# A mixture-of-experts step whose up product is turned over: stationary weights, moving rows, h born transposed

## The chip, the cores and the metric

The kernel runs on one core of a Trainium2 chip. The metric is the device time of one execution in microseconds. The times shown are the median of three runs; one more execution was profiled.

## What is computed

A decoder layer on x of shape (8, 256, 256) in three parts, each behind a layer norm and each added to x: a gated projection, a cross attention with a decay mask (retention), and a mixture of experts. The change touches the last part alone:

```python
xn = rms_norm(layernorm(x), norm_scale)              # 2048 tokens of 256
scores = xn @ w_router.T                             # 8 experts
ids = top_k(scores, 2); c = softmax(scores)[ids]
h = xn @ w_up[e].T                                   # 256 -> 1408, value and gate of 704
h = h_value * silu(h_gate)
y = h @ w_down[e].T                                  # 704 -> 256
out = x + sum over the 2 experts of y * c
```

## The kernel before

The stages run one after the other: stage A (projection), stage B (attention, norms, router scores, and beside them the scaling and splitting of the expert weights), the routing, and stage E, the experts. Stage E gathers the (token, expert) pairs, sorted by expert, into NSLOT = 39 tiles of 128 rows. All rows of a tile have one expert, whose number stands in `tile_e` and is only known on the chip.

Numbers are kept as a high and a low fp16 part. A product of two such numbers is made of three products (high by high, high by low, low by high); the list `products` holds them for the two halves c of the 256 inputs, so there are six matmuls for one output.

Stage E is a software pipeline, written out by hand for each engine in a function `step_e(it, k, r)`. `steps` unrolls steps 0 to 5 and 38 to 41, and puts steps 6 to 37 into a hardware loop whose body holds two steps (`E_STEPS`). In step r the up product is that of tile r-1, the down product that of tile r-2, and the y copy that of tile r-3. For one tile:

- GpSimd gathers the rows with an indirect DMA (L716), SyncE's queue transposes them with a DMA into `xsT`, which has two slots (L423).
- TensorE, up product (`up`, L1221): the transposed rows `xsT` are the stationary operand, the expert's weights `up_w` the moving one. Three groups fill bank 0 (gate, 512 columns), bank 1 (value, 512) and bank 2 (the last 192 gate and the last 192 value columns, 384). Each group is six matmuls. The rows of h come out on the partitions.
- ScalarE takes the silu of the gate (L608, L624), VectorE multiplies with the value (L1035), ScalarE makes the high fp16 part (L620, L626), VectorE the low one (L1041, L1043, L1044).
- TensorE transposes h in 11 pieces of 128x128 (L1251) into banks 4 and 5. VectorE copies eight of them (L1021) and ScalarE three (L614) to `hT`.
- TensorE, down product (L1276 to L1280): pieces of `hT` are stationary, the down weights `dn_w` moving, 256 columns, 17 matmuls in bank 7. Piece c has three products; the low part of the last 64 rows shares its piece with the high part.
- ScalarE scales y with the pair's weight (L602), and GpSimd adds it to the output with an indirect DMA (L726).

On TensorE the order within step r is: up group 0 of tile r-1, the transposes of tile r-2, up groups 1 and 2 of tile r-1, the down product of tile r-2.

Of the kernel before, what the change touches and what calls it, by code (L numbers as in the profile page):

```python
# [13 lines left out]
P = 128  # L14
NBATCH = 8
SEQ = 256
D = 256
# [40 lines left out]
def build(nc, x, ctxT, wproj, wproj2, w1, w2, gbias, wq, wk, wv, nscale, wr, wup, wdn, consts, consts_b, consts2, xrow_hbm, out):  # L58
# [5 lines left out]
    with ctx:  # L64
# [119 lines left out]
        def rt(n):  # L184
# [28 lines left out]
        sg = view(arena, 1728, H)  # L213
        hh = view(arena, 2432, H)
        hT = view(arena, 3136, H).bitcast(fp16).rearrange("p (c n) -> p c n", c=NHS)
        yt = view(arena, 3904, 2, D)
        hs = view(arena, 4416, H).bitcast(fp16)
        hs_high, hs_low_tail, hs_low4, hs_low = hs[:, 0:H], hs[:, H:H + HLAST], hs[:, H + HLAST:H + HLAST + P], hs[:, 2 * H - HA:2 * H]
        pair_scale = view(arena, 5120, NSLOT)
# [57 lines left out]
        s_trh, s_hTa, s_hTb = sem("h_transposed"), sem("hT_first_bank_ready"), sem("hT_second_bank_ready")  # L277
# [4 lines left out]

        hT_bank = [bank[4][:, :].bitcast(fp16).rearrange("p (c n) -> p c n", n=P),
                   bank[5][:, 0:3 * P // 2].bitcast(fp16).rearrange("p (c n) -> p c n", n=P)]
# [141 lines left out]
        def _(act):  # L426
# [165 lines left out]
            def step_e(it, k, r):  # L592
# [3 lines left out]
                if live(r, 3, NSLOT):  # L596
                    i, _, slot = at(it, k, 3)
                    act.wait_ge(s_y, i + 1)
                    act.wait_ge(s_ps, i + 1)
                    if r >= 5:  # L600
                        act.wait_ge(s_add, 16 * i - 16)
                    nc.scalar.activation(yt[:, slot], bank[7][:, 0:D], ACT.Copy, scale=pair_scale[:, ds(i, 1)]).then_inc(s_yt, 1)  # L602
                if live(r, 1, NSLOT):
# [4 lines left out]
                    nc.scalar.activation(sg[:, 0:HA], bank[0][:, 0:HA], ACT.Silu, scale=descale[:, ds(e, 1)]).then_inc(s_sg, 1)  # L608
                if live(r, 2, NSLOT):
                    i, _, _ = at(it, k, 2)  # L610
                    act.wait_ge(s_trh, i + 1)
                    if r >= 3:
                        act.wait_ge(s_y, i)
                    nc.scalar.activation(hT[:, 8:NHS], hT_bank[1], ACT.Copy).then_inc(s_hTb, 1)  # L614
                if live(r, 1, NSLOT):
                    i, _, slot = at(it, k, 1)
                    act.wait_ge(s_h, 2 * i + 1)
                    if r >= 2:
                        act.wait_ge(s_trh, i)
                    nc.scalar.activation(hs_high[:, 0:HA], hh[:, 0:HA], ACT.Copy).then_inc(s_hhi, 1)  # L620
# [3 lines left out]
                    nc.scalar.activation(sg[:, HA:H], bank[2][:, 0:HB], ACT.Silu, scale=descale2[:, ds(e, 1)]).then_inc(s_sg, 1)  # L624
                    act.wait_ge(s_h, 2 * i + 2)
                    nc.scalar.activation(hs_high[:, HA:H], hh[:, HA:H], ACT.Copy).then_inc(s_hhi, 1)  # L626
# [107 lines left out]
        def _(dve):  # L734
# [270 lines left out]
            V.tensor_copy(descale2, descale).then_inc(s_ysc, 1)  # L1005
            down_low(DN_TABLE, DN_GATHER)
            dve.wait_ge(s_ysc, 4)

            def step_e(it, k, r):
# [6 lines left out]
                if live(r, 2, NSLOT):  # L1016
                    i, _, _ = at(it, k, 2)
                    dve.wait_ge(s_trh, i + 1)
                    if r >= 3:
                        dve.wait_ge(s_y, i)  # L1020
                    V.tensor_copy(hT[:, 0:8], hT_bank[0]).then_inc(s_hTa, 1)  # L1021
# [5 lines left out]
                if live(r, 1, NSLOT):  # L1027

                    i, _, _ = at(it, k, 1)
                    for q, (src, cols) in enumerate(((bank[1][:, 0:HA], slice(0, HA)), (bank[2][:, HB:2 * HB], slice(HA, H)))):  # L1030
                        dve.wait_ge(s_sg, 2 * i + q + 1)
                        dve.wait_ge(s_up, 3 * i + q + 2)
                        if r >= 2:
                            dve.wait_ge(s_hlo, 2 * i + q - 1)
                        V.scalar_tensor_tensor(out=hh[:, cols], in0=src, scalar=h_scale[:, ds(e_h, 1)], in1=sg[:, cols],  # L1035
                                               op0=ALU.mult, op1=ALU.mult).then_inc(s_h, 1)
                        dve.wait_ge(s_hhi, 2 * i + q + 1)
                        if r >= 2 and q == 0:
                            dve.wait_ge(s_trh, i)
                        if q == 0:  # L1040
                            V.tensor_tensor(hs_low, hh[:, cols], hs_high[:, cols], ALU.subtract).then_inc(s_hlo, 1)  # L1041
                        else:
                            V.tensor_tensor(hs_low4, hh[:, HA:HA + P], hs_high[:, HA:HA + P], ALU.subtract)  # L1043
                            V.tensor_tensor(hs_low_tail, hh[:, HA + P:H], hs_high[:, HA + P:H], ALU.subtract).then_inc(s_hlo, 1)  # L1044
                    if r == 1:
                        down_low(DN_GATHER, 2 * NE)
# [4 lines left out]
        def _(pe):  # L1051
# [322 lines left out]
```

## Time and profile before

| | us |
|---|---|
| median of 3 runs | 443.6 (439.12 to 444.65) |
| the profiled execution, device time | 439.83 |
| its span, first to last instruction | 438.0 |
| first up matmul of stage E, from the span's start | 184.0 |
| TensorE busy | 365.9 (84% of the span) |
| VectorE busy | 269.9 (62%) |
| ScalarE busy | 236.5 (54%) |
| GpSimd busy | 191.2 (44%) |

The profile is that of one execution. Its span leaves out 1.8 us of the device time, which lie before the first and behind the last instruction. [...] Weight loads (PEld) run beside the matmuls. [...]

### The profile page before, as it was taken

What the parts mean: (1) busy time and instruction counts of PE and PEld (TensorE: products, weight loads), DVE (VectorE), ACT (ScalarE), POOL (GpSimd) and SP (SyncE); (2) the same over time, 40 slices, a digit from 0 to 9 for tenths busy, and PEclk for the clock granted to TensorE, in tenths of its full rate; (3) what the DMA queues carried; (4) which work ended last, traced back from release to release, by engine and by line L of the source; (5) the groups of instructions that cost most, each with busy time, mean ns of one, the idle gap of its engine ahead of it and who ended that gap; (6) DMA issues with size and microseconds to landing.
All of it is one profiled execution on the core that took longest, in us unless ns stands there. A gap on an engine that the chain in (4) does not pass through costs nothing.

```text
span 438.0 us, 9733 instructions
## 1 busy us (share of the span) xinstructions
PE 365.9 (84%) x2444; PEld 263.8 (60%) x2445; DVE 269.9 (62%) x688; ACT 236.5 (54%) x434; POOL 191.2 (44%) x186
## 2 busy tenths in 40 slices
PE   0899999788996411289999999999999999999980
PEld 0678888677885311056666666666666666666650
DVE  3698879978788899854445544455444554445530
ACT  3699877876765660534453444444445344444430
POOL 2544445866667413214333443334433444433321
PEclk9999999999998555599999999999999999999996
DMA  8999943352213170224343433434334343343420
GB/s 237 399 426 403 347 134 97 96 193 73 72 49 96 49 198 0 49 49 53 61 75 61 73 60 61 73 61 73 58 63 73 61 73 60 61 72 61 62 24 12
DMA packets 45859, 47.02 MB, mean 107 GB/s; under 512 B 26256, under 2 KB 41616, under 8 KB 44816
## 3 DMA queue, kind: packets, MB, share of 16 engines
q1 hardware_dynamic: 38304, 36.28, 26.5%
q0 software_dynamic: 7536, 10.52, 15.0%
q8 instruction: 8, 0.13, 0.1%
q14 instruction: 11, 0.09, 0.1%
HBM read 32.17 MB, written 9.50 MB: 95 GB/s over the span
## 4 chain that ended last, share of the span: by engine, by line
PE 70%; DVE 12%; issue 4%; ACT 4%; DMA 4%; SPq 1%; POOL 1%; DVEq 0%; ACTq 0%; POOLq 0%
PE bank L1225 32%; PE bank L1251 5%; PE bank L1276 5%; PE bank L1277 5%; PE bank L1278 5%; PE bank L1105 3%; PE bank L1153 3%; PE bank L1162 2%; DMA expert_w<-in_wup 2%; PE bank L1117 2%; ACT arena L438 2%; DVE expert_w L827 2%; DVE expert_w L836 1%; DVE arena L982 1%; PE bank L1058 1%
## 5 line engine op out<-in xcount | busy, mean ns | idle before, releaser
L1225 PE MATMUL bank<-expert_w,arena 128*128 x702 | 153.5, 364 | 8.8 <-DMA arena<-arena 8.6
L726 POOL DMA_INDIRECT out<-arena,add_idx x39 | 61.7, 1583 | 132.4 <-ACT arena L602 132.4
L1225 PEld LDWEIGHTS bank<-expert_w,arena 128*128 128x128 f16 x702 | 67.5, 98 | 68.0 <-issue 12.6
L1021 DVE COPY arena<-bank 128x1024 f16<-128x1024 f16 x39 | 27.0, 692 | 55.4 <-PE bank L1251 55.3
L620 ACT ACTIVATE arena<-arena 128x512 f16<-128x512 f32 x39 | 24.6, 630 | 64.8 <-DVE arena L1035 64.8
L1035 DVE SCALAR_TENSOR_TENSOR arena<-bank,dn_small,arena 128x512 f32<-128x512 f32 x78 | 45.4, 582 | 21.2 <-PE bank L1225 17.3
L1276 PE MATMUL bank<-expert_w,arena 128*128 x195 | 53.2, 273 | 1.3 <-DVE arena L1021 0.9
L1277 PE MATMUL bank<-expert_w,arena 128*128 x195 | 53.2, 273 | 0.0
L1278 PE MATMUL bank<-expert_w,arena 128*128 x195 | 53.2, 273 | 0.0
L716 POOL DMA_INDIRECT arena<-xrow_hbm,take_idx x39 | 38.9, 998 | 24.5 <-issue 11.5
L1041 DVE TENSOR_TENSOR arena<-arena 128x512 f16<-128x512 f32 x39 | 27.0, 693 | 27.1 <-ACT arena L620 27.1
L681 POOL TENSOR_TENSOR arena<-arena 128x512 f32<-128x512 f32 x16 | 27.0, 1689 | 21.4 <-DVE arena L864 15.5
L1251 PEld LDWEIGHTS bank<-ident,arena 128*128 128x128 f16 x429 | 27.1, 98 | 11.2 <-ACT arena L626 2.5
L602 ACT ACTIVATE arena<-bank,arena 128x256 f32<-128x256 f32 x39 | 18.5, 474 | 25.1 <-issue 20.6
L608 ACT ACTIVATE arena<-bank,small 128x512 f32<-128x512 f32 x39 | 26.8, 688 | 9.7 <-PE bank L1225 9.0
L827 DVE SCALAR_TENSOR_TENSOR expert_w<-expert_w,small 128x1408 f16<-128x1408 f32 (+1 forms) x16 | 30.3, 1893 | 2.6 <-ACT expert_w L483 1.2
L1251 PE MATMUL bank<-ident,arena 128*128 128x128 f16 x429 | 30.3, 219 | 1.8 <-DVE arena L1044 1.0
L626 ACT ACTIVATE arena<-arena 128x192 f16<-128x192 f32 x39 | 14.1, 363 | 30.3 <-DVE arena L1035 30.3
L1058 PE MATMUL bank<-cst,arena 128*128 128x128 f32 x96 | 16.7, 302 | 14.3 <-ACT arena L453 10.3
L507 ACT ACTIVATE expert_w<-expert_w,dn_small 128x768 f16<-128x768 f32 x16 | 14.7, 931 | 18.2 <-DVE expert_w L836 17.8
L438 ACT ACTIVATE arena<-expert_w,front 128x1408 bf16<-128x1408 f32 x16 | 23.7, 1479 | 1.0 <-DMA expert_w<-in_wup 0.8
L1058 PEld LDWEIGHTS bank<-cst,arena 128*128 128x128 f32 x96 | 12.4, 154 | 18.9 <-issue 11.3
(176 smaller groups left out, 673.5 us busy)
## 6 DMA issues: line engine op xcount, KB each, us to landing
expert_w<-in_wup SPq DMA_DIRECT2D x8, 1408.0 KB, 17.1
expert_w<-in_wdn SPq DMA_DIRECT2D x10, 640.0 KB, 5.0
rows<-in_x SPq DMA_DIRECT2D x8, 256.0 KB, 7.0
arena<-in_ctxT SPq DMA_DIRECT2D x8, 256.0 KB, 3.1
xrow_hbm<-front SPq DMA_DIRECT2D x8, 256.0 KB, 2.2
out<-rows SPq DMA_DIRECT2D x8, 256.0 KB, 2.8
expert_w<-in_wdn SPq DMA_DIRECT2D x20, 64.0 KB, 4.9
cst_b<-in_consts_b SPq DMA_DIRECT2D x1, 960.0 KB, 12.4
```

The lines of the kernel that those rows point to most:

```text
L438: nc.scalar.activation(squares, raw_chunk(e * 2 + c), ACT.Square, scale=ns_s[:, c:c + 1], accum_out=sq[:, ds(e * 2 + c, 1)]).then_inc(s_sq, 1)
L681: nc.gpsimd.tensor_tensor(dst[:, slot], dst[:, slot], rot[:, n], ALU.add).then_inc(rotated, 1)
L716: pool.indirect_dma_start(out=xs_row[:, i % 2], out_offset=None, in_=xrow_hbm, in_offset=bass.IndirectOffsetOnAxis(ap=take_idx[:, i:i + 1] ...
L726: pool.indirect_dma_start(out=out, in_=yt[:, i % 2], in_offset=None, out_offset=bass.IndirectOffsetOnAxis(ap=add_idx[:, i:i + 1], axis=0), ...
L827: V.scalar_tensor_tensor(out=part(n, 1), in0=raw_chunk(n), scalar=up_scale[:, ds(n, 1)], in1=part(n, 0), op0=ALU.mult, op1=ALU.subtract).t ...
L1035: V.scalar_tensor_tensor(out=hh[:, cols], in0=src, scalar=h_scale[:, ds(e_h, 1)], in1=sg[:, cols], op0=ALU.mult, op1=ALU.mult).then_inc(s_ ...
L1058: last = T.transpose(dst[:, c * SEQ + j * P:c * SEQ + (j + 1) * P], src(j, c), ident)
L1225: last = T.matmul(bank[q][:, 0:n], xsT[:, slot, 2 * a + c], up_w[:, ds(w0 + c * UPC + w * 2 * H + lo, n)], start=m == 0, stop=m == len(pro ...
L1251: last = T.transpose(hT_bank[c // 8][:, c % 8], hs[:, c * P:(c + 1) * P], ident16[:, :])
L1276: T.matmul(y, hT[:, c], dn_at(w_dn, c, 0), start=c == 0, stop=False)
L1277: T.matmul(y, hT[:, c], dn_at(w_dn, c, 1), start=False, stop=False)
L1278: T.matmul(y, hT[:, NH if c == NH - 2 else NH + 1 + c], dn_at(w_dn, c, 0), start=False, stop=False)
```

## The change

The up product is turned over. A tile of 128 weight columns of `up_w` is now the stationary operand, and the 128 rows of `xsT` move. Each output is 128 columns of h (on the partitions) by 128 rows, so h comes out transposed. There are twelve outputs for one tile: four in the gate bank, four in the value bank, and four in the third bank (128 gate columns, the last 64 gate columns, 128 value columns, the last 64 value columns), each of six matmuls as before. The transposes, banks 4 and 5 as their place, and the two copies out of them go. The high and low parts are written right into `hT`, which now has two slots. The up banks have two slots (0 to 2 and 3 to 5), y has two banks (6 and 7). The silu and the high part of the third bank take 256 columns in place of 192 (their last 64 partitions hold zeros or are not used). VectorE handles the last 128x192 product as one of 128x128 and one of 64x128, and the low part of the last tile is written to partitions 64 to 127. TensorE's order in step r becomes: all up groups of tile r-1, then the down product of tile r-2. The numbers of the computation and the weights' layout in memory are the same.

```diff
-            def up(i, slot, w0, q, lo, n, between=None):
+            def up_tile(q, slot, w0, t, columns):
                 for m, (c, a, w) in enumerate(products):
-                    if m == 3 and between:
-                        between()
-                    last = T.matmul(bank[q][:, 0:n], xsT[:, slot, 2 * a + c],
-                                    up_w[:, ds(w0 + c * UPC + w * 2 * H + lo, n)],
-                                    start=m == 0, stop=m == len(products) - 1)
-                last.then_inc(s_up, 1)
+                    weights = columns(w0 + c * UPC + w * 2 * H)
+                    last = T.matmul(bank[3 * slot + q][0:weights.shape[1], t * P:(t + 1) * P], weights,
+                                    xsT[:, slot, 2 * a + c], start=m == 0, stop=m == len(products) - 1)
+                return last
+
+            def whole(lo):
+                return lambda w0: up_w[:, ds(w0 + lo, P)]
+
+            def tail(lo):
+                return lambda w0: up_w[:, ds(w0 + lo + P, HLAST)]
...
-                    if r >= 2:
-                        pe.wait_ge(s_h, 2 * i - 1)
-                    up(i, slot, w_up, 0, 0, HA)
+                    if r >= 3:
+                        pe.wait_ge(s_h, 2 * i - 2)
+                    for q in range(2):
+                        for t in range(HA // P):
+                            last = up_tile(q, slot, w_up, t, whole(q * HA + t * P))
+                        last.then_inc(s_up, 1)
+                    if live(r, 2, NSLOT):
+                        load_expert("down", at(it, k, 2)[0], 2 * DNC)
+                    for t, columns in enumerate((whole(2 * HA), tail(2 * HA), whole(2 * HA + HB), tail(2 * HA + HB))):
+                        last = up_tile(2, slot, w_up, t, columns)
+                    last.then_inc(s_up, 1)
                 if live(r, 2, NSLOT):
-                    i, _, _ = at(it, k, 2)
-                    pe.wait_ge(s_hhi, 2 * i + 2)
-                    pe.wait_ge(s_hlo, 2 * i + 2)
-                    if r >= 3:
-                        pe.wait_ge(s_hTa, i)
-                        pe.wait_ge(s_hTb, i)
-                    for c in range(NHS):
-                        last = T.transpose(hT_bank[c // 8][:, c % 8], hs[:, c * P:(c + 1) * P], ident16[:, :])
-                    last.then_inc(s_trh, 1)
...
-                    pe.wait_ge(s_hTa, i + 1)
-                    pe.wait_ge(s_hTb, i + 1)
-                    if r >= 3:
-                        pe.wait_ge(s_yt, i)
-                    y = bank[7][:, 0:D]
+                    pe.wait_ge(s_hhi, 2 * i + 2)
+                    pe.wait_ge(s_hlo, 2 * i + 2)
+                    if r >= 4:
+                        pe.wait_ge(s_yt, i - 1)
+                    y = bank[6 + slot][:, 0:D]
```

On ScalarE and VectorE:

```diff
-                    nc.scalar.activation(hT[:, 8:NHS], hT_bank[1], ACT.Copy).then_inc(s_hTb, 1)
...
-                    nc.scalar.activation(hs_high[:, 0:HA], hh[:, 0:HA], ACT.Copy).then_inc(s_hhi, 1)
+                    nc.scalar.activation(hT_high[slot][:, 0:HA], hh[:, 0:HA], ACT.Copy).then_inc(s_hhi, 1)
...
-                    nc.scalar.activation(sg[:, HA:H], bank[2][:, 0:HB], ACT.Silu, scale=descale2[:, ds(e, 1)]).then_inc(s_sg, 1)
+                    nc.scalar.activation(sg[:, HA:NH * P], bank[3 * slot + 2][:, 0:2 * P], ACT.Silu,
+                                         scale=descale2[:, ds(e, 1)]).then_inc(s_sg, 1)
...
-                    V.tensor_copy(hT[:, 0:8], hT_bank[0]).then_inc(s_hTa, 1)
...
+                    V.scalar_tensor_tensor(out=hh[:, whole], in0=bank[3 * slot + 2][:, 2 * P:3 * P], scalar=h_scale[:, ds(e_h, 1)],
+                                           in1=sg[:, whole], op0=ALU.mult, op1=ALU.mult)
+                    V.scalar_tensor_tensor(out=hh[0:HLAST, tail], in0=bank[3 * slot + 2][0:HLAST, 3 * P:4 * P],
+                                           scalar=h_scale[0:HLAST, ds(e_h, 1)], in1=sg[0:HLAST, tail],
+                                           op0=ALU.mult, op1=ALU.mult).then_inc(s_h, 1)
...
+                    V.tensor_tensor(hT_low[slot][:, whole], hh[:, whole], hT_high[slot][:, whole], ALU.subtract)
+                    V.tensor_tensor(hT[HLAST:P, slot, NH - 1], hh[0:HLAST, tail], hT[0:HLAST, slot, NH - 1],
+                                    ALU.subtract).then_inc(s_hlo, 1)
```

## Rows read from the trace of the kernel before

**Rows 1.** The page, parts 1 and 2: TensorE's busy time; its clock in 40 slices
```profile
PE 365.9 (84%) x2444; PEld 263.8 (60%) x2445; DVE 269.9 (62%) x688; ACT 236.5 (54%) x434; POOL 191.2 (44%) x186
...
PEclk9999999999998555599999999999999999999996
```

**Rows 2.** Windows: stretch and length, busy us (instructions) by engine, PEclk, DMA, GB/s
```profile
70.00:80.00 10.00, 7.57 (x39) 6.08 (x37) 9.57 (x23) 6.84 (x9) 6.74 (x7) 1.00 0.01 2
...
130.00:140.00 10.00, 7.03 (x41) 6.11 (x41) 9.13 (x20) 5.48 (x8) 7.56 (x8) 0.99 0.33 105
140.00:150.00 10.00, 4.29 (x18) 3.34 (x16) 8.86 (x15) 4.98 (x10) 6.55 (x6) 0.50 0.15 52
...
210.00:400.00 190.00, 189.59 (x1442) 125.33 (x1441) 91.65 (x217) 88.22 (x188) 79.98 (x63) 1.00 0.38 66
```

**Rows 3.** Groups of instructions, 210 to 400 us: count, busy us, mean ns, idle before
```profile
L1225 PE MATMUL bank<-expert_w,arena 128*128 x563 | 122.1, 362 | 0.0
L1225 PEld LDWEIGHTS bank<-expert_w,arena 128*128 128x128 f16 x562 | 53.6, 98 | 45.9 <-issue 1.1
...
L1251 PE MATMUL bank<-ident,arena 128*128 128x128 f16 x352 | 24.9, 219 | 0.0
...
L1021 DVE COPY arena<-bank 128x1024 f16<-128x1024 f16 x31 | 21.4, 692 | 46.6 <-PE bank L1251 46.6
...
L614 ACT ACTIVATE arena<-bank 128x384 f16<-128x384 f16 x31 | 15.0, 483 | 0.0
```

**Rows 4.** Timeline of one step, 300.3 to 306.5 us: start, length, what, how many
```profile
300.46 1.46 PE L1225 MATMUL bank<-expert_w,arena 128*128 x6
...
301.75 0.78 PE L1251 MATMUL bank<-ident,arena 128*128 128x128 f16 x11
...
302.37 2.43 PE L1225 MATMUL bank<-expert_w,arena 128*128 x12
...
304.63 0.27 PE L1276 MATMUL bank<-expert_w,arena 128*128 x1
...
306.38 0.27 PE L1280 MATMUL bank<-expert_w,arena 128*128 x1
...
306.49 1.46 PE L1225 MATMUL bank<-expert_w,arena 128*128 x6
```

**Rows 5.** Line L1225, 183.8 to 185.4 us: count, min/median/max ns, first and last start
```profile
L1225 PEldq FUSED_REGOPS  x12: 46/46/46, 183.9 to 185.3; - x12
...
L1225 PE MATMUL bank<-expert_w,arena x4: 606/634/634, 184.0 to 185.3; 128*128 x4
```

**Rows 6.** Line L1276, 305.1 to 305.8 us, the down product within the step of rows 4
```profile
L1276 PEldq FUSED_REGOPS  x3: 46/46/46, 305.1 to 305.6; - x3
L1276 PEld LDWEIGHTS bank<-expert_w,arena x2: 95/96/98, 305.2 to 305.5; 128*128 128x128 f16 x2
```

**Rows 7.** Lines L1225, L1276, L1279 and L1280, 210 to 400 us
```profile
L1225 PEldq FUSED_REGOPS  x375: 46/46/51, 210.1 to 400.0; - x188
...
L1276 PEldq FUSED_REGOPS  x155: 46/46/60, 212.2 to 395.7; - x155
...
L1279 PEldq FUSED_REGOPS  x31: 46/46/46, 213.5 to 395.9; - x31
...
L1280 PE MATMUL bank<-expert_w,arena x31: 272/273/273, 215.0 to 397.7; 128*128 x31
```

**Rows 8.** L1219, 304.2 to 305.2; then L1219, L1249, L310, 210 to 400 us
```profile
L1219 PEldq FUSED_REGOPS  x2: 46/98/151, 304.3 to 304.8; - x2
...
L1219 PEldq TENSOR_LOAD <-arena x63: 297/303/630, 210.3 to 399.3; - x63
...
L1249 PEldq EVENT_SEMAPHORE  x31: 51/485/507, 215.6 to 398.3; - x31
...
L310 PEldq COMPARE_BRANCH  x15: 207/208/220, 225.8 to 396.3; - x15
```

**Rows 9.** Line L1280 over the whole span: the last matmul of the kernel
```profile
L1280 PE MATMUL bank<-expert_w,arena x39: 272/273/273, 196.9 to 426.4; 128*128 x39
```

More of the change, by code:

```diff
@@ L212, in build @@
         xsT = view(arena, 1120, 2, 2 * P).bitcast(fp16).rearrange("p s (c n) -> p s c n", c=4)
[L213 to L219, printed above, removed]
+        sg = view(arena, 1728, NH * P)
+        hh = view(arena, 1728 + NH * P, NH * P)
+        hT = view(arena, 1728 + 2 * NH * P, 2 * H).bitcast(fp16).rearrange("p (s c n) -> p s c n", s=2, c=NHS)
+        hT_low = [hT[:, s, NH:NHS].rearrange("p c n -> p (c n)") for s in range(2)]
+        hT_high = [hT[:, s, 0:NH].rearrange("p c n -> p (c n)") for s in range(2)]
+        o = 1728 + 2 * NH * P + 2 * H
+        yt = view(arena, o, 2, D)
+        pair_scale = view(arena, o + 2 * D, NSLOT)
+        assert o + 2 * D + NSLOT <= 5840 and (NH - 1) * P + HLAST == H
         bank = [ctx.enter_context(nc.psum_tensor(f"bank{i}", [P, 512], fp32)) for i in range(8)]
@@ L276, in build @@
         s_hhi, s_hlo = sem("h_high_ready"), sem("h_low_ready")
-        s_trh, s_hTa, s_hTb = sem("h_transposed"), sem("hT_first_bank_ready"), sem("hT_second_bank_ready")
         s_y, s_yt = sem("y_ready"), sem("y_copied")
@@ L601, in step_e @@
                         act.wait_ge(s_add, 16 * i - 16)
-                    nc.scalar.activation(yt[:, slot], bank[7][:, 0:D], ACT.Copy, scale=pair_scale[:, ds(i, 1)]).then_inc(s_yt, 1)
+                    nc.scalar.activation(yt[:, slot], bank[6 + slot][:, 0:D], ACT.Copy, scale=pair_scale[:, ds(i, 1)]).then_inc(s_yt, 1)
                 if live(r, 1, NSLOT):
@@ L1005, in _ @@
             V.tensor_copy(descale2, descale).then_inc(s_ysc, 1)
+            V.memset(hh[HLAST:P, (NH - 1) * P:NH * P], 0.0)
             down_low(DN_TABLE, DN_GATHER)
@@ L1027, in step_e @@
                 if live(r, 1, NSLOT):
[L1029 to L1044, printed above, removed]
@@ new lines, in step_e @@
+                    i, _, slot = at(it, k, 1)
+                    tail = slice((NH - 1) * P, NH * P)
+                    whole = slice(HA, (NH - 1) * P)
+                    dve.wait_ge(s_sg, 2 * i + 1)
+                    dve.wait_ge(s_up, 3 * i + 2)
+                    if r >= 2:
+                        dve.wait_ge(s_hlo, 2 * i - 1)
+                    V.scalar_tensor_tensor(out=hh[:, 0:HA], in0=bank[3 * slot + 1][:, 0:HA], scalar=h_scale[:, ds(e_h, 1)],
+                                           in1=sg[:, 0:HA], op0=ALU.mult, op1=ALU.mult).then_inc(s_h, 1)
@@ new lines, in step_e @@
+                    dve.wait_ge(s_hhi, 2 * i + 1)
+                    V.tensor_tensor(hT_low[slot][:, 0:HA], hh[:, 0:HA], hT_high[slot][:, 0:HA], ALU.subtract).then_inc(s_hlo, 1)
+                    dve.wait_ge(s_sg, 2 * i + 2)
+                    if r >= 2:
+                        dve.wait_ge(s_hlo, 2 * i)
+                    V.scalar_tensor_tensor(out=hh[:, whole], in0=bank[3 * slot + 2][:, 2 * P:3 * P], scalar=h_scale[:, ds(e_h, 1)],
+                                           in1=sg[:, whole], op0=ALU.mult, op1=ALU.mult)
@@ L1275, in step_e @@
                             load_expert("up", at(it, k, 0)[0], 2 * UPC)
-                        T.matmul(y, hT[:, c], dn_at(w_dn, c, 0), start=c == 0, stop=False)
-                        T.matmul(y, hT[:, c], dn_at(w_dn, c, 1), start=False, stop=False)
-                        T.matmul(y, hT[:, NH if c == NH - 2 else NH + 1 + c], dn_at(w_dn, c, 0), start=False, stop=False)
-                    T.matmul(y, hT[:, NH - 1], dn_at(w_dn, NH - 1, 0), start=False, stop=False)
-                    T.matmul(y, hT[:, NH - 1], dn_at(w_dn, NH - 1, 1), start=False, stop=True).then_inc(s_y, 1)
+                        T.matmul(y, hT[:, slot, c], dn_at(w_dn, c, 0), start=c == 0, stop=False)
+                        T.matmul(y, hT[:, slot, c], dn_at(w_dn, c, 1), start=False, stop=False)
+                        T.matmul(y, hT[:, slot, NH + c], dn_at(w_dn, c, 0), start=False, stop=False)
+                    T.matmul(y, hT[:, slot, NH - 1], dn_at(w_dn, NH - 1, 0), start=False, stop=False)
+                    T.matmul(y, hT[:, slot, NH - 1], dn_at(w_dn, NH - 1, 1), start=False, stop=True).then_inc(s_y, 1)
             steps(pe, step_e, *E_STEPS)
```

34 lines of the change are left out of this document (4 added, 30 removed).

## The prediction

> **What bounds the kernel now.** I read the page first, then the windows, then the groups of stage E, and last one step in the timeline. TensorE is the busiest engine, 365.9 of 438.0 us, and its clock is full but for one stretch before stage E [rows 1]. From 210 to 400 us it is busy for 189.59 of 190.00 us, while VectorE (91.65) and ScalarE (88.22) are busy under half the time [rows 2]. No up matmul there has idle time before it, and the 46.6 us for which VectorE waited for the transposes before L1021 are slack of an engine that nobody waits for [rows 3]. So in stage E every microsecond is TensorE's array.
>
> One step, from starts to starts [rows 4]: six up matmuls from 300.46 to 301.75 (1.29), eleven transposes to 302.37 (0.62), twelve up matmuls to 304.63 (2.26), seventeen down matmuls to 306.49 (1.86). Sum 6.03 us. Over 30 steps the last down matmul goes from 215.0 to 397.7 us [rows 7], 6.09 each. The reader should take the price of one matmul from these: 128 moving columns cost (0.78 - 0.219) / 10 = 0.056 us, each transpose with a weight load of its own [rows 3, 4]; 256 columns cost (306.38 - 304.63) / 16 = 0.109.
>
> **The array's side of the change.** The up product becomes 12 outputs by 6 products = 72 matmuls of 128 moving columns, 72 x 0.056 = 4.03 us, in place of 1.29 + 2.26 = 3.55. The transposes (0.62) go, the down product (1.86) stays. 4.03 + 1.86 = 5.89 us against 6.03: 0.14 us less in each step, some 5 us over 38 steps. If the array stays the bound, this is all that can be won; the waits at the start and the end of the pipeline would add a little.
>
> **The sequencer's side.** Each weight address comes from a register, and the trace shows what that costs. Before the first up groups the sequencer works through 12 FUSED_REGOPS between 183.9 and 185.3 us, in which time the array starts only four matmuls [rows 5]: it doesn't wait for the array, and takes 1.4 / 11 = 0.127 us for one, though its own record is 46 ns. In the down product L1276's three start at 305.1 to 305.6 with one of L1277 between each two: 0.5 / 4 = 0.125 [rows 6]. The two weight loads of L1276 there start 0.1 us behind their address instructions, so for a moment the array is already fed no faster than the sequencer computes. I take 0.125 us, bounds 0.12 and 0.13.
>
> How many are there? L1225 has 375 of them for 563 matmuls [rows 7], two for three matmuls: the six products use four different addresses (two halves, high and low part), and the third product of each half uses that of the first again. It has three groups in a step, so 12. The down product has 5 at L1276 (155 in 31 steps), 5 at L1277, 1 at L1279 and 1 at L1280 [rows 7], again one for each different address. Together 24 a step, 24 x 0.125 = 3.0 us, hidden behind 6.03 us of array.
>
> After the change each of the twelve outputs has its own column offset: 12 x 4 = 48 addresses, and 12 in the down product as before. 60 x 0.125 = 7.5 us a step. Nothing in the trace shows a register address on a weight load, since today all of them in this stage are on moving operands. I take the same price, as the address is computed in the same instruction ahead of it; nothing for the pair itself, as L1278 has no address instruction and the 0.125 us hold with its pair in between [rows 6].
>
> What else the sequencer does in a step: two loads of an expert number. One runs from 304.3 [rows 8] to the next address instruction at 305.1 [rows 6], 0.8 us; those of median length (303 ns) would be a bit under, 0.75. So 1.5 for two. The loop's branch is 0.21 in every second step [rows 8]. With the waits, whose cost no row gives singly: all of it is at least 1.6, and at most 6.09 - 3.0 - 0.43 = 2.66, because for 485 - 51 ns the sequencer only stands at L1249 [rows 8]. I take 2.4 for today. The change takes away the waits ahead of the transposes and ahead of the third group, for which I take 0.3 off: 2.1 (1.5 to 2.4).
>
> The sum for a step is 7.5 + 2.1 = 9.6 us, against 5.89 of the array. The sequencer becomes the bound, and the array goes hungry: 3.5 us more than 6.09 in each step. The bounds are 60 x 0.12 + 1.5 = 8.7 and 60 x 0.13 + 2.4 = 10.2.
>
> **The other engines.** VectorE loses the copy of 0.692 and gains two short instructions, each under the 0.483 that 384 columns cost at L614; ScalarE loses those 0.483 and gains two times 64 columns [rows 3]. At 91.65 / 31 = 3.0 and 88.22 / 31 = 2.8 us a step [rows 2] neither binds at 5.9 or at 9.6. The chain that is now behind the down product (silu, product, high and low part of the third bank: some five instructions on at most 256 columns, at under 0.483 each at most 2.4 us) has the previous down product, or in the steady state a whole up product of 6 us, as cover. At nothing, then; without the cover it would cost its 2.4 us less the 1.9 of the down product. The row gathers and transposes by DMA run two tiles ahead of a pace that only gets slower.
>
> **The sum.** Stage E begins at 184.0 us [rows 5], unchanged. First tile, up only: at the half clock that holds there (four matmuls of 512 columns start 1.3 / 3 = 0.43 apart [rows 5], twice the 0.216 of full clock), 0.107 a matmul, array bound, 7.2 us with part of it at full clock. Then 38 steps at 9.6, less 0.3 for the six outside the loop (no branch, no loop counter): 363. The last step has only a down product, 1.9 with 0.3 of waiting. The end of its matmuls falls at 184.0 + 7.2 + 363 + 2.2 = 556.4. Today 426.4 + 0.3 = 426.7 [rows 9] is followed by 11.3 us to the end (copy of y, scatter, landing), which stay: 567.7 of span. With the 1.8 us around the span 569.5. The profiled execution had 439.8 where the median of the runs is 443.6, 0.9% more; I put about a third of this on top: 571 us. With the bounds of the step, 38 x -0.9 and 38 x +0.6, the likeliest case has 538 to 594.
>
> **Rivals.** (a) The array's clock falls. It would be fed for 5.89 of 9.6 us, in bits. For it: from 130 to 140 us TensorE was busy for 7.03 of 10 us, and at its end the clock fell to half; against it: from 70 to 80 us it was busy for 7.57 of 10 at full clock [rows 2], and the records of 219 ns at a spacing of at most 125 would leave gaps only at the expert loads, some 1.1 us of 9.6. At half clock all the time the array needs twice 5.89, 11.7 us, more than the sequencer's 9.6: 38 x 2.1 = 80 more, 650 us. More likely it would go to and fro, as a slow array is a full one: 580 to 640, middle 610.
>
> (b) The other side: the address instructions don't bind. A build could find fewer than 48 addresses, or they could cost less where no profile is taken. It decides from (5.89 - 2.1) / 60 = 0.063 us for one instruction, or at 30 instructions of 0.125 a step. Then the array rules with 5.89, the time falls by 5 us and by 2 to 3 more at the pipeline's two ends: 435 us, right at the edge of what can be told from no change. Against it: 24 different addresses have 24 instructions in the trace, and the array was short of work at 305.2 us already.
>
> (c) More instructions than I count: each of the 72 stationary operands has its own, because weight loads don't share. 84 x 0.125 + 2.1 = 12.6 a step, 38 x 3.0 = 114 more: 685 us.
>
> (d) The array is slower at short matmuls than eleven transposes show, since these may have been lined up ahead. [...]
>
> **Chances.** Sequencer bound at full clock 0.72 (571); (a) 0.14 (610); (b) 0.08 (435); (c) 0.04 (685); (d) alone 0.02 (504). A measurement of this kernel tells about 2% from no change, so (b) is half faster and half the same: faster 0.04, same 0.04, slower 0.92. The range holds the likeliest case and most of (a): 540 to 635.
>
> **What the changed profile would show.** In the steady stretch: 48 FUSED_REGOPS a step at the up product's line, 0.125 us apart; weight loads with idle time put down to issue, several us a step; steps of 9.6 us; TensorE's records still near full, but VectorE and ScalarE under a third; PEclk at full. [...]

## The result and the profile after

The changed kernel takes 578.8 us (median of 4 runs, 578.5 to 582.8), the kernel before 442.8 beside it. The ratio is 1.311, with a 95% interval of 1.300 to 1.321. The forecast was 571 us, 540 to 635.

The page of the changed kernel, its span, parts 1, 2 (the clock in 40 slices) and 4 (the chain of work that ended last), and two groups of part 5. The last line is part 4 of the page of before:

```profile
span 576.9 us, 14190 instructions
...
PE 458.4 (79%) x4121; PEld 359.4 (62%) x4122; DVE 263.2 (46%) x689; ACT 230.6 (40%) x395; POOL 190.9 (33%) x186
...
PEclk9999999999555999999999999999999999999996
...
PE 71%; issue 11%; DVE 7%; ACT 5%; DMA 2%; POOL 1%; SPq 1%; DVEq 0%; ACTq 0%; POOLq 0%
...
L1217 PE MATMUL bank<-arena,expert_w 128*128 128x128 f16 (+1 forms) x2808 | 253.4, 226 | 44.5 <-issue 35.9
L1217 PEld LDWEIGHTS bank<-arena,expert_w 128*128 (+1 forms) x2808 | 194.2, 99 | 105.1 <-issue 56.9
```

```profile
PE 70%; DVE 12%; issue 4%; ACT 4%; DMA 4%; SPq 1%; POOL 1%; DVEq 0%; ACTq 0%; POOLq 0%
```

PEclk is the granted TensorE clock as a share of full speed. It is what it was: 9 tenths or more in nearly all slices, with a dip to 5 in both kernels that is over soon after stage E begins [rows 1], and 1.00 from 210 to 400 us in both [rows 2]. What has grown is the word issue: 11% of the chain in place of 4%, and 35.9 us of idle time ahead of the up matmuls, where [rows 3] show none in the steady stretch of before. Issue is time in which an engine waited for nothing that the profile shows another engine do. Here it is TensorE's own sequencer that is late, as the address instructions below show, 0.129 us apart without a pause.

The same windows as in [rows 2] (stretch and length; busy us and instructions of PE, PEld, DVE, ACT, POOL; clock; DMA share; GB/s), and the timeline over one step of the changed kernel:

```profile
210.00:400.00 190.00, 165.65 (x1729) 125.30 (x1727) 53.19 (x134) 51.65 (x96) 51.05 (x40) 1.00 0.24 41
```

```profile
306.43 0.47 ACT L600 ACTIVATE arena<-bank,arena 128x256 f32<-128x256 f32 x1 [0.77 <-PE bank L1264]
306.90 4.10 PEld L1217 LDWEIGHTS bank<-arena,expert_w 128*128 x48 [1.13 <-issue]
306.90 4.27 PE L1217 MATMUL bank<-arena,expert_w 128*128 128x128 f16 x48 [0.85 <-issue]
...
309.35 0.69 ACT L606 ACTIVATE arena<-bank,small 128x512 f32<-128x512 f32 x1 [2.44 <-PE bank L1217]
```

TensorE starts 1729 matmuls in the stretch, VectorE falls from 91.65 to 53.19 us busy and ScalarE from 88.22 to 51.65: in part the copies that went, above all fewer steps. The records of matmuls overlap: eleven transposes of 219 ns each are over in 0.78 us [rows 3, 4]. So the price of a matmul is read from start to start. The array stands for 0.85 us ahead of this group, while the sequencer takes the loop's branch and reads an expert's number; the other reads of a number leave it idle for 0.4 to 0.6 us. The 48 up matmuls of the first two banks then take (4.27 - 0.22) / 47 = 0.086 each, not the 0.056 of the transposes of before.

The sequencer's own instructions at the up product's line, over these 48 matmuls; over 220 to 540 us; and the last down matmul of each step from 220 to 525 us:

```profile
L1217 PEld LDWEIGHTS bank<-arena,expert_w x48: 95/96/99, 306.9 to 310.9; 128*128 x48
L1217 PE MATMUL bank<-arena,expert_w x48: 219/227/228, 306.9 to 311.0; 128*128 128x128 f16 x48
L1217 PEldq FUSED_REGOPS  x32: 46/46/46, 306.8 to 310.8; - x32
...
L1217 PEldq FUSED_REGOPS  x1570: 46/46/51, 220.0 to 539.2; - x197
...
L1264 PE MATMUL bank<-expert_w,arena x31: 272/272/273, 227.0 to 521.7; 128*128 x31
```

32 address instructions for 48 matmuls, 4.0 / 31 = 0.129 us apart, without a pause: this is the sequencer at its own pace, and the array follows it: from 220 to 520 us a weight load starts 0.095 us behind the start of an address in 1201 of 1473 cases. Six products have four addresses, so half of the addresses serve one matmul and half serve two, and by the single starts in the trace the next address comes 0.124 us later after either. So in this stream one more pair of weight load and matmul adds nothing to the distance that can be seen; the address sets it. A step is (521.7 - 227.0) / 30 = 9.82 us on average, and 1570 addresses in 320 us are 48 for each. Long steps (10.7) and short ones (8.9) alternate, because the first step of the loop's body has three of the four reads of an expert's number and the branch. Before, a step was 6.09 [rows 7].

That FUSED_REGOPS at an operand's line are its address from a register, three runs show. In the kernel before, L1219 reads the expert's number with 63 TENSOR_LOAD, 303 ns at the median, from 210 to 400 us [rows 8]; L1225, whose moving operand lies in the expert's weights, has 375 address instructions for 563 matmuls [rows 7]; and L1251, whose operands have addresses fixed at build time, has none for 352 matmuls. In the changed kernel, where the expert's weights are stationary, L1217 has 1570 for 2358 matmuls from 220 to 540 us. In a_fixed_up, where this line has constants in their place, it has none for 2094 matmuls from 215 to 400 us.

### The profile page after: what moved, and what is told of

It reads as the page before. It is cut to its first block, busy times and chain, and to the rows that moved or that the text cites. A ratio compares the mean times of both kernels' runs of the same rounds, so it can differ in the third digit from the quotient of the medians.

```text
span 576.9 us, 14190 instructions
## 1 busy us (share of the span) xinstructions
PE 458.4 (79%) x4121; PEld 359.4 (62%) x4122; DVE 263.2 (46%) x689; ACT 230.6 (40%) x395; POOL 190.9 (33%) x186
## 4 chain that ended last, share of the span: by engine, by line
PE 71%; issue 11%; DVE 7%; ACT 5%; DMA 2%; POOL 1%; SPq 1%; DVEq 0%; ACTq 0%; POOLq 0%
PE bank L1217 43%; PE bank L1260 5%; PE bank L1261 4%; PE bank L1262 4%; PE bank L1098 3%; PE bank L1146 2%; ACT arena L436 2%; PE bank L1155 2%; PE bank L1110 1%; ACT arena L451 1%; PE bank L1051 1%; DVE expert_w L825 1%; PE bank L1059 1%; DVE expert_w L816 1%; DVE arena L971 1%
## 5 line engine op out<-in xcount | busy, mean ns | idle before, releaser
L1217 PE MATMUL bank<-arena,expert_w 128*128 128x128 f16 (+1 forms) x2808 | 253.4, 226 | 44.5 <-issue 35.9
L1217 PEld LDWEIGHTS bank<-arena,expert_w 128*128 (+1 forms) x2808 | 194.2, 99 | 105.1 <-issue 56.9
L1021 DVE SCALAR_TENSOR_TENSOR arena<-bank,dn_small,arena 128x512 f32<-128x512 f32 x39 | 29.3, 751 | 134.2 <-PE bank L1217 132.9
L1260 PE MATMUL bank<-expert_w,arena 128*128 x195 | 53.6, 275 | 11.3 <-issue 9.5
L1261 PE MATMUL bank<-expert_w,arena 128*128 x195 | 53.6, 275 | 0.0
L1262 PE MATMUL bank<-expert_w,arena 128*128 x195 | 53.2, 273 | 0.0
L612 ACT ACTIVATE arena<-bank,dn_small 128x256 f32<-128x256 f32 x39 | 18.5, 475 | 47.2 <-PE bank L1217 47.2
L1260 PEld LDWEIGHTS bank<-expert_w,arena 128*128 128x128 f16 x195 | 18.9, 97 | 23.8 <-issue 21.5
L1029 DVE SCALAR_TENSOR_TENSOR arena<-bank,dn_small,arena 128x128 f32<-128x128 f32 x39 | 13.7, 351 | 38.8 <-ACT arena L612 38.8
L1009 DVE TENSOR_TENSOR arena<-arena,dn_small (+1 forms) x39 | 6.3, 161 | 47.0 <-issue 47.0
L615 ACT ACTIVATE arena<-arena 128x256 f16<-128x256 f32 x39 | 16.2, 416 | 26.1 <-DVE arena L1031 26.1
```

Source lines behind the costliest of these rows:

```text
L1021: V.scalar_tensor_tensor(out=hh[:, 0:HA], in0=bank[3 * slot + 1][:, 0:HA], scalar=h_scale[:, ds(e_h, 1)], in1=sg[:, 0:HA], op0=ALU.mult, o ...
L1217: last = T.matmul(bank[3 * slot + q][0:weights.shape[1], t * P:(t + 1) * P], weights, xsT[:, slot, 2 * a + c], start=m == 0, stop=m == len ...
L1260: T.matmul(y, hT[:, slot, c], dn_at(w_dn, c, 0), start=c == 0, stop=False)
L1261: T.matmul(y, hT[:, slot, c], dn_at(w_dn, c, 1), start=False, stop=False)
L1262: T.matmul(y, hT[:, slot, NH + c], dn_at(w_dn, c, 0), start=False, stop=False)
```

## The experiments

All are compared with the kernel before on the same chip. The step is the mean of 30 in the hardware loop (an even number, as long and short ones alternate), taken between their last down matmuls. In short:

| kernel | addresses a step | step, us | median, us | ratio to before (95%) |
|---|---|---|---|---|
| before | 24 | 6.09 | 439 to 443 | 1 |
| changed | 60 | 9.82 | 578.8 | 1.300 to 1.321 |
| a_72_addresses | 84 | 12.79 | 698.9 | 1.579 to 1.598 |
| a_extra_load | 60, one load more | 10.53 | 609.1 | 1.376 to 1.394 |
| a_short_addresses | 60, 48 of them short | 9.26 | 558.3 | 1.260 to 1.281 |
| a_32_addresses | 44, 8 of them short | 7.76 | 499.3 | 1.128 to 1.145 |
| a_fixed_up | 12 | 6.32 | 448.6 | 1.013 to 1.029 |
| a_grouped | all, in 15 instructions | 6.33 | 449.0 | 1.014 to 1.027 |
| a_grouped_wide | as a_grouped | 5.88 (5.93 with one step of 7.47) | 433.2 | 0.978 to 0.994 |
| a_one_tail | all, in 14 instructions | 5.69 | 425.8 | 0.961 to 0.975 |
| b_35_addresses | 35 | 6.84 | 468.9 | 1.054 to 1.073 |
| b_grouped | all, grouped | 6.04 | 440.2 | 0.996 to 1.004 |

### Is it the number of addresses? a_fixed_up, a_32_addresses, a_72_addresses, a_extra_load

The theory is the prediction's: a step is the larger of the array's work and the sequencer's, and the sequencer's is 0.128 us for each address and some 2.1 for the rest. The rivals: the array is slow at many short matmuls; or a wait elsewhere took the place of the transposes.

a_fixed_up:

```diff
-                    w_up = expert["up"]
+                    w_up = 0
```

> The changed kernel, but every up product takes the weights of expert 0, at addresses fixed when the program is built; the choice of the expert in the up product is left out. All matmuls, weight loads, waits and the down product's 12 address instructions stay. Theory (sequencer): 48 of the 60 address instructions of a step go, 9.86 - 48 x 0.128 = 3.7 us of sequencer work, so the array binds at 5.89 us a step: 9.86 - 5.89 = 3.97 less over 38 steps, 151 us off 579: 428 to 436 us. [...] Rival (chain behind the down product, or another wait): the time stays near 579.

a_32_addresses:

```diff
-                            last = up_tile(q, slot, w_up, t, whole(q * HA + t * P))
+                            last = up_tile(q, slot, w_up, t, whole(q * HA + t // 2 * 2 * P))
...
-                    for t, columns in enumerate((whole(2 * HA), tail(2 * HA), whole(2 * HA + HB), tail(2 * HA + HB))):
+                    for t, columns in enumerate((whole(2 * HA), tail(2 * HA - P), whole(2 * HA + HB), tail(2 * HA + HB - P))):
```

> The changed kernel, but neighbouring outputs of a bank take the same weight columns (the second of each pair computes the first again; half of the h columns are left out), so a step has 32 up addresses in place of 48, 8 of these in the short form of a single register operation (0.09 us). Matmuls and weight loads are as many as before. Theory (sequencer): 16 x 0.128 + 8 x 0.035 = 2.3 us less a step, 38 x 2.3 = 88 off: 491 us. Rivals (array or a wait elsewhere): 579, as nothing changes for the array.

a_72_addresses:

```diff
-                    weights = columns(w0 + c * UPC + w * 2 * H)
+                    weights = columns(w0 + c * UPC + w * 2 * H + 2 * a)
```

> The changed kernel, but the third product of each half takes weights two columns further on, so each of the 72 up matmuls has an address of its own (its result is wrong in a third of the products). Theory (sequencer): 24 more address instructions, 24 x 0.128 = 3.07 us a step, 38 x 3.07 = 117 more: 696 us. Rivals (array, wait): 579.

a_extra_load:

```diff
                     if live(r, 2, NSLOT):
+                        load_expert("spare", at(it, k, 2)[0], 2 * DNC)
                         load_expert("down", at(it, k, 2)[0], 2 * DNC)
```

> The changed kernel with one more load of an expert number (never used) in each step, 0.75 us of sequencer work with its arithmetic. Theory (sequencer): 38 x 0.75 = 28.5 more, 607 us: whatever the sequencer does is on the path, not only addresses. Rivals (array, wait elsewhere): under 5 us more, as the load is hidden behind the array's queue.

Measured: 448.6, 499.3, 698.9 and 609.1 us, where the theory said 428 to 436, 491, 696 and 607, and the rivals 579 for most. Three of the four are within 9 us. The step of a_72_addresses is 9.82 + 24 x 0.128 = 12.89 by the sum and 12.79 by the trace. (The expectations above take 9.86 for the changed kernel's step, which is the mean of 31 steps, one long one too many.) The array has the same matmuls in a_32_addresses, the changed kernel, a_72_addresses and a_extra_load, so neither rival has a place for 200 us between them. In the last two its granted clock was in part lower (0.85 to 0.87 and 0.89 to 0.95 in the windows of stage E, last section); that doesn't set the step, which follows the count of instructions. Even a load that nobody uses shows in full: 10.53 - 9.82 = 0.71 us a step where 0.75 were expected.

a_fixed_up is 13 to 20 us over its forecast. Timeline of its step, TensorE only, from the last down matmul of one step to the first of the next, and its groups from 215 to 400 us by shape:

```profile
304.72 0.27 PE L1264 MATMUL bank<-expert_w,arena 128*128 x1
...
304.82 4.52 PE L1217 MATMUL bank<-arena,expert_w 128*128 128x128 f16 x72
...
309.28 0.28 PE L1260 MATMUL bank<-expert_w,arena 128*128 x1
```

```profile
L1217 PE MATMUL bank<-arena,expert_w 128*128 128x128 f16 x1746 | 107.4, 219 | 0.0
...
L1217 PE MATMUL bank<-arena,expert_w 128*64 128x128 f16 x348 | 30.3, 223 | 0.0
```

No idle time is left, so the array binds here, but 72 matmuls take 309.28 - 304.82 = 4.46 us in place of 4.03. By the starts of single matmuls in the same trace nearly all stand 0.056 apart; those at which the stationary operand goes from 128 to 64 columns or back stand 0.15 apart, and there are four of these in a step (116 in 29 steps), each with one of 0.065 to 0.12 behind it. That is the 0.43. a_grouped_wide, below, tests it.

### Is it what an address costs? a_short_addresses, a_grouped

An address is formed from a column number, by the author's count in three register operations (add the offset, times two bytes, add the base); the trace has one instruction for it, FUSED_REGOPS with a record of 46 ns. Formed in bytes, it is one addition, an ALU_OP of 32 ns in this run's trace:

```diff
+        up_b = expert_w[:, 0:NE * UPC].bitcast(mybir.dt.uint8)
...
-                    weights = columns(w0 + c * UPC + w * 2 * H)
+                    weights = columns(w0 + 2 * (c * UPC + w * 2 * H))
...
-                return lambda w0: up_w[:, ds(w0 + lo, P)]
+                return lambda w0: up_b[:, ds(w0 + 2 * lo, 2 * P)].bitcast(fp16)
```

(`load_expert` scales by bytes too, and `tail` in the same way.)

> The changed kernel, same results and same number of instructions, but the 48 up addresses of a step are formed in bytes, so that each is one register addition (the short record, about 0.092 us from start to start in the trace of the changed kernel) in place of the fused instruction of three operations (0.128). Sequencer theory: 48 x 0.035 = 1.7 us less a step, 38 x 1.7 = 65 off: 514 us. Rival (the stream of instructions itself, or fetching them, sets the pace whatever they do): 579. Rival (array or a wait): 579.

It took 558.3 us, a gain of 21 where 65 were expected. The record of an address is shorter, 32 ns in place of 46:

```profile
L1218 PEldq ALU_OP  x940: 32/32/36, 217.5 to 399.9; - x188
```

but the distance between two is 0.116 on average in place of 0.128, not 0.092: that value was for an addition with a semaphore instruction behind it (L1252 of the changed kernel), not a matmul. 48 x 0.012 = 0.58 us a step; 9.82 - 9.26 = 0.56 were measured. So by these two forms most of the price, 0.116 of 0.128, is that of an instruction, whatever it computes. The direction fits the sequencer, the size was misjudged.

The rival of this run, that fetching the program sets the pace, is not settled by a_fixed_up or a_grouped, which both have a shorter program. The DMA queues of the changed kernel settle it. Over its whole span its page shows two queues for instructions; in a stretch of its loop there is none:

```profile
q8 instruction: 13, 0.21, 0.2%
q14 instruction: 11, 0.09, 0.1%
```

```profile
q0 software_dynamic: 2067, 2.81, 17.2%
q1 hardware_dynamic: 5984, 1.44, 6.8%
```

The first two lines are the page's, the others are all queues from 245 to 350 us. The steps are 9.82 us there too, with nothing fetched.

a_grouped takes the consequence: with one addition for each address, the four of an output fit into one fused instruction, if they are formed ahead of the six matmuls.

```diff
             def up_tile(q, slot, w0, t, columns):
+                for c in range(2):
+                    for w in range(2):
+                        pe.lower_ap(columns(w0 + 2 * (c * UPC + w * 2 * H)), for_matmul_weights=True)
...
                     for c in range(NH - 1):
+                        if c % 3 == 0:
+                            for cc in range(c, c + 3):
+                                pe.lower_ap(dn_bytes(w_dn, cc, 0))
+                                pe.lower_ap(dn_bytes(w_dn, cc, 1))
```

> The changed kernel, same results, with byte addresses that are computed four at a time ahead of each up output (12 fused instructions in place of 48 a step) and six at a time in the down product. Sequencer theory: about 12 x 0.14 + 2 x 0.2 + 2.2 = 4.3 us of sequencer a step, hidden; the array binds. The run with fixed up addresses (448.6 us, steps of 6.32 us) is the same for the array, so 446 to 450 us here. If the gain of fixed addresses came from anything else than the sequencer (less program, all tiles reading one expert's weights), this run stays above 500.

It took 449.0 us, as a_fixed_up. Its address instructions at the up product and its up matmuls of one step:

```profile
L1218 PEldq FUSED_REGOPS  x351: 55/55/74, 215.9 to 399.4; - x176
...
305.00 4.52 PE L1221 MATMUL bank<-arena,expert_w 128*128 128x128 f16 x72
```

351 in 183.5 us are 12 in each step of 6.33 us; one with four additions lasts 55 ns, 9 more than the three operations of before. All matmuls, loads and waits of the changed kernel are in this run, each tile reads its own expert's weights, and 130 of its 136 us of loss are gone. With the stretch without fetches this shows the cause.

### What is left: a_grouped_wide, a_one_tail

a_grouped_wide:

```diff
-                return lambda w0: up_b[:, ds(w0 + 2 * lo + 2 * P, 2 * HLAST)].bitcast(fp16)
+                start = lo + P - (HLAST if lo > 2 * HA else 0)
+                return lambda w0: up_b[:, ds(w0 + 2 * start, 2 * P)].bitcast(fp16)
```

> As a_grouped, but the 64 tail columns are loaded as 128 (the gate tail with 64 columns too many, whose outputs nobody reads; the value tail starts 64 columns early, so that its 64 h columns are left out and wrong ones take their place). Number and size of matmuls are the same. In the run with fixed addresses each change between 128 and 64 weight columns had matmuls 0.15 apart in place of 0.056, four times a step, and some smaller ones: 4.46 us for 72 matmuls in place of 4.03. Theory (the short weight loads cost that): 0.43 less a step, 38 x 0.43 = 16 off: 432 us. Rival (it is the change of bank or group that costs): as a_grouped, 448.

433.2 us, and steps of 5.88. The number of matmuls, their moving columns and the order of banks are those of a_grouped, so the operands of 64 columns among those of 128 did cost 0.45 us a step, 16 us in all. Such a matmul also writes 64 partitions in place of 128; which of the two has the price, the weight load or the output, no run shows.

a_one_tail puts the two tails side by side:

```diff
-    w_up = np.concatenate([gate[:, :HA], value[:, :HA], gate[:, HA:], value[:, HA:]], 1)
+    w_up = np.concatenate([gate[:, :HA], value[:, :HA], gate[:, HA:HA + P], value[:, HA:HA + P],
+                           gate[:, HA + P:], value[:, HA + P:]], 1)
...
-                    for t, columns in enumerate((whole(2 * HA), tail(2 * HA), whole(2 * HA + HB), tail(2 * HA + HB))):
+                    for t, columns in ((0, whole(2 * HA)), (1, whole(2 * HA + 2 * P)), (2, whole(2 * HA + P))):
...
+                    nc.scalar.activation(sg[HLAST:P, HA + P:NH * P], bank[3 * slot + 2][0:HLAST, P:2 * P], ACT.Silu,
+                                         scale=descale2[0:HLAST, ds(e, 1)]).then_inc(s_sg, 1)
...
-                                           scalar=h_scale[0:HLAST, ds(e_h, 1)], in1=sg[0:HLAST, tail],
+                                           scalar=h_scale[HLAST:P, ds(e_h, 1)], in1=sg[HLAST:P, tail],
```

> As a_grouped, same results, with the last 64 gate and the last 64 value columns side by side in the weights' layout, so that they are one tile of 128: 66 up matmuls in place of 72, no weight load of 64 columns. ScalarE takes the tail's silu in an instruction of its own (0.35 us) that writes it to partitions 64 to 127, beside the values. Theory: array 66 x 0.056 + 1.86 = 5.56 us a step; 6.04 in the kernel before; 38 x 0.48 = 18 less than before: 422 us (ratio 0.96). Rival (with a shorter step something else binds, as the chain from the scatter's landing to the next one or the row gathers): steps of 5.8 to 6.0 and 430 to 438 us.

425.8 us, ratio 0.968 (0.961 to 0.975): with the results of the kernel before, and faster than both. The step is 5.69, between theory (5.56) and rival (5.8). Its groups and waits from 215 to 390 us name where the 0.13 go:

```profile
L1223 PE MATMUL bank<-arena,expert_w 128*128 128x128 f16 x2026 | 118.4, 219 | 2.7 <-DMA arena<-arena 2.0 <-issue 0.7
L1223 PEld LDWEIGHTS bank<-arena,expert_w 128*128 x2024 | 115.2, 98 | 4.9 <-issue 4.3
```

2.7 us over 31 steps stand in the open, 2.0 of them two waits for the transposing DMA of the rows. That is 0.09 a step. The rest hides in the records: a down matmul's record lasts 0.27 us at a spacing of 0.109, so each pause is 0.16 us longer than the idle time shown. By the starts of single matmuls 19 of 30 steps take 5.54 us, what the theory says. The others have eleven pauses, six ahead of the up product (3.6 us) and five in the down product at the read of an expert's number (0.8 us): 4.5 / 30 = 0.15 us a step. So of the rival only the row transposes are in it, and now and then.

### Does it hold for the kernel before? b_35_addresses, b_grouped

b_35_addresses:

```diff
-                                    up_w[:, ds(w0 + c * UPC + w * 2 * H + lo, n)],
+                                    up_w[:, ds(w0 + c * UPC + w * 2 * H + lo + 2 * a, n)],
...
-                        T.matmul(y, hT[:, NH if c == NH - 2 else NH + 1 + c], dn_at(w_dn, c, 0), start=False, stop=False)
+                        T.matmul(y, hT[:, NH if c == NH - 2 else NH + 1 + c], dn_at(w_dn + 2, c, 0), start=False, stop=False)
```

> The kernel before, with the third product of each half (up) and of each piece (down) reading weights two columns further on, so that each of the 35 matmuls with a moving weight has its own address: 35 address instructions a step in place of 24; the low parts' products take wrong columns. The array's work is the same. Sequencer theory: the kernel before has 2.4 + 24 x 0.125 = 5.4 us of sequencer in a step of 6.09, so room for five more instructions; with eleven more it is 5.4 + 11 x 0.128 = 6.8 us and binds: 38 x 0.7 = 27 more than 440, 467 us. Rival (the sequencer's time matters only in the turned-over order, where weight loads wait for it): 440.

b_grouped is the kernel before with byte addresses, `pe.lower_ap` of the four weights ahead of each up group, and of six ahead of each half of the down product.

> The kernel before, same results, with byte addresses computed four (up) and six (down) at a time. The array's step is 6.03 by the sum of its matmuls, 6.09 were measured, the difference being short waits for the sequencer. Theory: 38 x 0.06 = 2.3 us less, 437: the same within what can be told. Then the gain of the version with one tail over the kernel before comes from the turned-over product and not from the cheaper addresses. Rival: cheaper addresses are worth over 2% by themselves (under 431).

468.9 and 440.2 us. Line L1225 of b_35_addresses, from 215 to 400 us, with its idle time:

```profile
L1225 PEldq FUSED_REGOPS  x486: 46/46/51, 217.2 to 398.6; - x162
L1225 PEld LDWEIGHTS bank<-expert_w,arena x486: 95/98/98, 217.3 to 399.2; 128*128 128x128 f16 x162
...
  issue: 28.1, 41
```

Eleven more addresses put the old order over the edge as well, at the place that the sum gave: 6.84 us a step measured, 6.8 expected. So the kernel before ran with 0.6 us of room in its sequencer, and this isn't a matter of stationary or moving operands. b_grouped shows that freeing the sequencer is worth nothing that can be told where the array binds (0.9999, 0.996 to 1.004; the step goes from 6.09 to 6.04). The 3.2% of a_one_tail come from the turned-over product with its tails in one tile; the cheap addresses only let it be seen.

## Why the prediction was right, point by point

**What bounds before:** right. b_grouped puts the array at 6.04 us a step, b_35_addresses the sequencer at 6.84 - 11 x 0.128 = 5.4.

**The count of 60 addresses:** right, 48 at L1217 as counted and 12 in the down product. That a weight load's register address costs what a moving operand's does was an assumption; it holds (0.128 in the changed kernel against 0.125 to 0.127 in the kernel before).

**The price of one:** 0.125 was taken from two short stretches, inside the bounds of 0.12 and 0.13. Over the whole changed kernel it is 0.128: most stand 0.124 apart, and every eighth or so 0.155. 60 x 0.003 = 0.18 us a step. This is most of the miss of 8 us: the step was to be 9.6 and is 9.82, 38 x 0.22 = 8.4.

**The start and the end:** two small errors that nearly cancel. The up product of stage E began at 182.9 us and not at 184.0, and the first down product was done some 2 us sooner than the sum has it. The end, which was to stay at 11.3 us, took 13.4: the last scatter now waits for the landing of the one before it, which had begun only 1.6 us before the last down matmul. In the chain that ended last:

```profile
561.61 4.01 DMA out<-arena,add_idx
...
566.38 1.55 POOL out L715
```

The sum for the range has a slip too: 38 x 0.9 is 34, so the likeliest case begins at 537, not 538. Nothing hangs on it.

**The rest of the sequencer's step, 2.1:** 9.82 - 60 x 0.128 = 2.1. Right, and one load costs 0.71 by a_extra_load, where 0.75 was read. That the waits which go are worth 0.3 was a guess; b_35_addresses has 6.84 - 35 x 0.128 = 2.4 for the kernel before, so it was a good one.

**The array's side, 5.89:** wrong, and hidden. The rows for it were transposes with 128 columns each. 5.89 + 0.43 for the operands of 64 columns is the 6.32 of a_fixed_up. The change would have cost 2% even with free addresses, since 6.32 is over 6.09. Rival (b), free addresses and 435 us, would have come out at 449: on the slower side, not on the faster. Nothing in the trace of before has a weight load of 64 columns; this was an operation without a row, and the prediction gave it no bounds. It did no harm here because the sequencer's side is 3.5 us longer; where the two sides are close, an error of this size decides.

**The other engines at nothing:** right but for the end. In the steady stretch of the changed kernel every one of them waits for TensorE (VectorE is busy for 53.19 of 190.00 us, and 132.9 us of the idle time ahead of its 39 products at L1021 end with a matmul of L1217), and in a_grouped too, at 6.3 us a step (TensorE 190.00, VectorE 82.02, ScalarE 80.20 of 190.00 us).

**Rival (a), a falling clock:** did not happen in the changed kernel (1.00 in the windows), though the array had 6.3 us of work in steps of 9.82 us. In the two runs with longer steps it fell in part, as the last section shows, and cost nothing that the sum leaves open, because the sequencer binds.

**Rival (c), an address for each product:** refuted by the count. a_72_addresses is that case built, and its 699 us are near the 685 given for it.

**Rival (d), 0.08 for a short matmul in a long stream:** refuted. In a_grouped_wide the up matmuls stand 0.056 apart:

```profile
304.05 2.62 PE L1221 MATMUL bank<-arena,expert_w 128*128 128x128 f16 x44
```

(2.62 - 0.22) / 43 = 0.056, with a weight load for each matmul (2256 loads for 2258 matmuls from 215 to 400 us). The 504 us of this rival take 0.08 us for each matmul. No run shows that term as the pace of a stream; what the runs showed in its place is 0.056, the price read from the eleven transposes. Distances of 0.08 stand in a_fixed_up only behind a change from 128 to 64 columns, two in a step.

## What to carry to other kernels

Cost a change on both sides of TensorE: the array by moving columns, and its sequencer by instructions, where a register address is one (here 0.128 us, against 0.056 for a matmul of 128 columns). The second did not show in the busy times of the kernel before (TensorE 189.59 of 190.00 us) and could be read beforehand from its queue's records (twelve addresses 0.127 us apart [rows 5]). It turned over here with 72 small matmuls at 48 addresses that depend on data: 9.82 us a step, where the array needs 6.32. Count different addresses, form them in the unit that the address needs, and several ahead, so that they share an instruction (a_grouped: 12 of 55 ns in place of 48, and steps of 6.33). And keep weight loads of 64 columns out of a stream of 128 (they cost 0.45 us a step in a_grouped), or put two halves side by side.

## What was not expected of the hardware

In a_fixed_up and a_grouped, changing between stationary operands of 128 and 64 columns costs about 0.1 us each time (0.15 between starts in place of 0.056), with no wait in the profile to show for it (idle time 0.0 ahead of the up matmuls). The longest record of an up matmul there is 243 ns in place of 219, and the weight load's is 110 in place of 98. So 64 columns load no faster than 128 in these runs: the record of their load is 106 to 110 ns, of 128 columns 95 to 99.

An instruction that computes one addition costs the sequencer 0.116 us between matmuls (a_short_addresses) where one with three operations costs 0.128 (the changed kernel) and one with four additions at least 0.133 (the shortest distance of two in a_grouped): the arithmetic is nearly free there, the instruction isn't.

In the two runs with the longest steps the granted clock fell in part. Windows of a_72_addresses (steps of 12.8 us) over its stage E:

```profile
300.00:400.00 100.00, 93.58 (x692) 69.59 (x692) 22.11 (x56) 21.12 (x40) 18.58 (x15) 0.85 0.18 31
400.00:500.00 100.00, 93.99 (x698) 69.91 (x698) 21.64 (x54) 20.55 (x39) 19.99 (x16) 0.86 0.18 31
```

0.85 is a mean of stretches at full and at half clock: the window from 304.7 to 308.0 us has 0.50, that from 308.1 to 318.3 has 1.00. It fell though TensorE's records cover 94% of the time: an up matmul's record is 0.228 us long at the median and most of their starts are 0.124 us apart, so a record covers pauses too. With steps of 10.5 us (a_extra_load) the clock was 0.93 to 0.95 in windows of 100 us from 200 to 500 us, in the changed kernel 1.00 from 210 to 400 us. The busy time of a hungry array says little about how much it does: 692 matmuls fill 93.58 of 100 us here, 2782 fill 187.30 of 190 in a_one_tail.
